# A two-layer decoder on one core: the last layer's first batch moved into the attention's pair loop, and two orders of the first layer changed

## The chip, the cores and the metric

One core of a Trainium2 chip runs the whole kernel in one launch. TensorE (PE) multiplies, VectorE (DVE), ScalarE (ACT) and GpSimd (POOL) work element by element, and SyncE (SP) starts the DMAs. Each engine takes its own instructions strictly in order, and they meet at semaphores. The metric is the time of one execution in device microseconds. Smaller is better.

## The reference, cut to what matters

The stream `x` is (2, 512, 128) in float32: two batches of 512 tokens, 1024 rows, kept as 8 tiles of 128 rows. Six sublayers follow one another, each with a residual sum and a layer norm:

```python
x = ln(x + gated_mix(x))                        # first layer, "a"
x = ln(x + cross_attention_and_ssm(x, ctx_768)) # "b": top 32 of 154 scores, FiLM, S4D by DFT, an FFN
x = ln(x + mha_and_moe(x))                      # "c": 8 experts, capacity 128
x = ln(x + attention(x))                        # last layer, "d": 16 heads of 64 in each batch, no mask
x = ln(x + latent_attention(ctx_768, x, mask))  # "e": 2 heads of 64, keys = 154 of the context + 512 of x
x = ln(x + top2_ffn(x))                         # "f": 4 live experts, hidden size 704

# d, in each batch:   z = softmax(q k^T / 8) v over 16 heads; y = x + concat(z) w_o
# e, in each batch:   ln_l = ln(x) * g + b; q, k, v = ln_l Wq^T, ln_l Wlkv^T;  the context gives 154 more k, v
#                     q, k: each head's row divided by its root mean square, times a gain
#                     softmax over 666 keys (masked ones of the context out), times v, times Wo^T, + bo
```

## The kernel before, in words

All data of a stage lies in SBUF at addresses planned by hand; `Space` hands out stretches and later stages reuse them. PSUM has 8 banks of 512 float32 columns, and `bank(i)` is bank i. The order on each engine is the order of the program text, and every hand-over is a named semaphore: `wait_ge(sem(name), n)` waits until it was raised n times. There is no planner.

**The first layer's b stage (L637 to L1060).** ScalarE writes angles in turns for the state-space kernel: 32 low lags and 16 high lags for each channel. VectorE rounds them (`b_dve_rounds`, L482 and L484), GpSimd subtracts (`b_pool_low_angles` in two halves, `b_pool_high_angles`), ScalarE takes the sine and cosine (`b_act_high_waves`, `b_act_low_waves`). Beside this, VectorE selects the 32 largest of 154 scores in 16 steps of two heads, and ScalarE feeds it with exponentials (`exponentials(j)`). GpSimd starts `b_pool_attention` with seven small operations on the FiLM row (`b_pool_film_rows`), then the marks, both low halves, the high angles, `u_n`, and then factors and modulated tiles in turn. `b_act_film_inputs` copies four products from PSUM between two exponentials. `taps_of_lags` on TensorE needs all factors, and everything of the state-space part follows it.

**The c stage (L1220 to L1525).** After the norm of the attention's output, the rows are transposed in two halves (`half_turn`), `logits` gives the gate, VectorE finds each row's expert, and `count_before` counts the rows ahead of it for the capacity. `expert(t)` multiplies tile t by all eight merged experts, in two halves of four experts each, `bias(t)` adds the biases, and `combine` on VectorE adds 128x128 blocks by their coefficients: 16 for two tiles. `rows_again(h)` turns the rows back, ScalarE copies them to `moe_sum`. GpSimd adds `n2_b` to the stream (`with_n2b`, L1432) right after the two reciprocal roots of the norm.

**The d stage (L1539 to L1817).** A pair is two heads of one batch; there are NP_ = 16, pairs 0 to 7 in batch 0. Step i of the loop holds the scores and exponentials of pair i, the rough maxima of pair i+1 (bf16 products whose row maximum becomes the shift of the exponent, written into a row of its own, `shift_in`), the projections of pair i+2, and the weighing and sums of pair i-1. Scores use banks 0 to 3, rough maxima 4 and 5, weighing 6, and projections and sums share bank 7. VectorE reduces four rough maxima, writes the shift row, takes the reciprocal of the sums (`unit`) and scales the weighed pair into `headed`. GpSimd adds the exponentials over keys (two half sums and a key sum for each pair). Step 16 only drains. Steps 14 and 15 also hold the turn and the product of the normed context. Behind the loop stand 64 products of the output projection, 8 pairs for each of 8 tiles (L1706).

**The e stage (L1821 to L2205).** Batch 0 first: residual sum and norm, a second norm, four transpositions, four latent projections of 384 columns, the norms of q and k rows (squares from ScalarE, `square_sums` and `scale` on VectorE, the power -1/2 on GpSimd, L1870), transpositions of q and k, casts to bf16, four rough maxima of 666 keys in four banks (1332 columns read), shift, then six chunks of scores and weighing. Batch 1's norm, projections, turns and maxima are put between batch 0's steps. The f stage's products start when the sums of batch 1 are on TensorE's queue (`hide`, L2243); their weights (4352 KB) come by a DMA that waits for the e stage's first stream norm, since they overwrite `value`.

## Time and profile before

| | |
|---|---|
| three runs | 701.97, 703.33, 707.58 us; median 703.33 |
| the profiled execution | 701.16 us, its span 699.4 us |
| TensorE, matmul | 614.9 us busy, 88% of the span |
| TensorE, weight load | 310.2 us, 44%, beside the matmuls |
| VectorE | 442.6 us, 63% |
| ScalarE | 288.4 us, 41% |
| GpSimd | 251.8 us, 36% |
| mean granted clock of TensorE | 0.943 of full speed |

A float32 product of a 128x512 tile is two matmul records. The granted clock is 1.00 or 0.50, which are 2.4 and 1.2 GHz. The chain that ended last is TensorE for 60% of the span, VectorE for 20%, GpSimd for 11%. The b stage runs to about 160 us, the c stage to 235, the d stage's loop starts at 249.6, the output projection at 470.6, and the f stage's first product at 555.9.

### The profile page before, as it was taken

What the parts mean: (1) busy time and instruction counts of PE and PEld (TensorE: products, weight loads), DVE (VectorE), ACT (ScalarE), POOL (GpSimd) and SP (SyncE); (2) the same over time, 40 slices, a digit from 0 to 9 for tenths busy, and PEclk for the clock granted to TensorE, in tenths of its full rate; (3) what the DMA queues carried; (4) which work ended last, traced back from release to release, by engine and by line L of the source; (5) the groups of instructions that cost most, each with busy time, mean ns of one, the idle gap of its engine ahead of it and who ended that gap; (6) DMA issues with size and microseconds to landing.
All of it is one profiled execution on the core that took longest, in us unless ns stands there. A gap on an engine that the chain in (4) does not pass through costs nothing.

```text
span 699.4 us, 8759 instructions
## 1 busy us (share of the span) xinstructions
PE 614.9 (88%) x3153; PEld 310.2 (44%) x3153; DVE 442.6 (63%) x1170; ACT 288.4 (41%) x548; POOL 251.8 (36%) x180
## 2 busy tenths in 40 slices
PE   7764869999797989999999999988568999999996
PEld 4322557876563322222222222328222346665655
DVE  6997997457739746676677667646743773333234
ACT  7969967032320564444444444420423342212120
POOL 2794652332601526446544554642435100000001
PEclk9956979999988999999999999999969999999998
DMA  8200014030000000000000000000600000000001
GB/s 319 88 0 0 2 66 178 1 121 1 1 0 1 0 0 1 1 0 1 1 1 1 0 1 0 1 1 0 256 0 1 0 1 1 0 1 0 1 0 31
DMA packets 3681, 18.92 MB, mean 27 GB/s; under 512 B 917, under 2 KB 2198, under 8 KB 3126
## 3 DMA queue, kind: packets, MB, share of 16 engines
q1 hardware_dynamic: 3638, 18.36, 6.9%
q8 instruction: 25, 0.41, 0.2%
q14 instruction: 18, 0.15, 0.1%
HBM read 17.84 MB, written 0.52 MB: 26 GB/s over the span
## 4 chain that ended last, share of the span: by engine, by line
PE 60%; DVE 20%; POOL 11%; issue 5%; ACT 4%; POOLq 0%; DVEq 0%; ACTq 0%
PE PS L2243 10%; PE PS L1607 8%; PE PS L2257 6%; DVE SB L1781 6%; PE PS L1591 5%; PE PS L1552 4%; PE PS L1575 3%; POOL SB L238 2%; PE PS L1623 2%; DVE SB L212 2%; DVE SB L199 2%; PE PS L1965 2%; DVE SB L1503 1%; PE PS L1976 1%; POOL SB L516 1%
## 5 line engine op out<-in xcount | busy, mean ns | idle before, releaser
L1767 POOL TENSOR_TENSOR SB<-SB 128x1024 f32<-128x1024 f32 x32 | 75.2, 2350 | 108.1 <-ACT SB L1730 108.0
L1781 DVE TENSOR_REDUCE SB<-PS 128x2 f32<-128x1024 f32 x64 | 78.5, 1226 | 55.0 <-PE PS L1575 54.9
L1730 ACT ACTIVATE SB<-PS 128x1024 f32<-128x1024 f32 x64 | 65.5, 1023 | 101.8 <-PE PS L1594 101.7
L2243 PE MATMUL PS<-SB 128*128 128x512 f32 x176 | 83.1, 609 | 0.2 <-DVE SB L2320 0.2
L1591 PE MATMUL PS<-SB 64*128 64x512 f32 x256 | 68.9, 616 | 1.1 <-ACT SB L1734 1.1
L1607 PE MATMUL PS<-SB 128*64 128x512 f32 x256 | 67.8, 610 | 1.2 <-DVE SB L1815 1.2
L2295 ACT ACTIVATE SB<-PS 128x512 f32<-128x512 f32 (+1 forms) x48 | 28.5, 595 | 92.0 <-PE PS L2243 89.0
L1811 DVE RECIPROCAL SB<-PS 128x512 f32<-128x512 f32 x16 | 53.7, 3358 | 17.6 <-PE PS L1623 17.6
L238 POOL TENSOR_TENSOR SB<-SB 128x4 f32<-128x4 f32 x18 | 19.6, 1092 | 120.9 <-DVE SB L204 120.9
L2320 DVE TENSOR_TENSOR SB<-SB,PS 128x512 f32<-128x512 f32 (+1 forms) x48 | 32.7, 687 | 48.1 <-PE PS L2243 43.7
L2257 PEld LDWEIGHTS PS<-SB 128*128 128x128 f32 (+1 forms) x384 | 49.4, 190 | 18.5 <-issue 10.0
L2257 PE MATMUL PS<-SB 128*128 128x128 f32 (+1 forms) x384 | 54.5, 285 | 1.4 <-DVE SB L2320 1.4
L244 POOL TENSOR_TENSOR SB<-SB 128x4 f32<-128x4 f32 (+1 forms) x6 | 5.5, 920 | 132.4 <-DVE SB L182 132.2
L2243 PEld LDWEIGHTS PS<-SB 128*128 128x128 f32 x176 | 31.1, 190 | 33.0 <-issue 27.7
L1552 PE MATMUL PS<-SB 128*128 128x512 f32 x64 | 37.5, 673 | 1.2 <-ACT SB L1713 0.7
L1771 POOL TENSOR_TENSOR SB<-SB 128x1024 f32<-128x1024 f32 x16 | 37.6, 2348 | 1.3
L1591 PEld LDWEIGHTS PS<-SB 64*128 64x128 f32 x256 | 22.0, 188 | 28.3 <-issue 23.5
L1607 PEld LDWEIGHTS PS<-SB 128*64 128x64 f32 x256 | 14.3, 135 | 42.8 <-issue 33.0
L2351 DVE SCALAR_TENSOR_TENSOR SB<-PS,SB 128x128 f32<-128x128 f32 x32 | 11.2, 351 | 30.3 <-PE PS L2257 30.3
L1575 PE MATMUL PS<-SB 64*128 64x512 bf16 x128 | 24.8, 384 | 4.6 <-DVE SB L1781 4.6
L1575 PEld LDWEIGHTS PS<-SB 64*128 64x128 bf16 x128 | 6.2, 93 | 47.0 <-DVE SB L1781 40.4
L1722 ACT ACTIVATE SB<-PS 128x512 bf16<-128x512 f32 x32 | 19.1, 597 | 17.5 <-PE PS L1552 17.5
(392 smaller groups left out, 1131.6 us busy)
## 6 DMA issues: line engine op xcount, KB each, us to landing
SB<-exp SPq DMA_DIRECT2D x1, 4352.0 KB, 13.8
SB<-moe SPq DMA_DIRECT2D x1, 4096.0 KB, 12.2
SB<-dft SPq DMA_DIRECT2D x1, 2304.0 KB, 11.7
SB<-att SPq DMA_DIRECT2D x1, 2048.0 KB, 7.9
SB<-mix SPq DMA_DIRECT2D x1, 768.5 KB, 4.4
SB<-mix SPq DMA_DIRECT2D x1, 640.0 KB, 5.5
SB<-ssm SPq DMA_DIRECT2D x1, 602.0 KB, 6.6
SB<-lat SPq DMA_DIRECT2D x1, 585.0 KB
```

Source lines behind the costliest of these rows:

```text
L238: pool.tensor_tensor(rstd[:, a:z], variance[:, a:z], minus_half[:, a:z], ALU.pow).then_inc(sem("norm_rstd"), 1)
L1552: pe.matmul(bank(b), w[:, 128 * pair:128 * pair + 128], xsT[:, 512 * batch:512 * batch + 512], start=True, stop=True)\
L1575: ins = pe.matmul(bank(4 + h), qb_ring[i % 3][head(h), 128 * qt:128 * qt + 128], kb_ring[i % 3][head(h), :], start=True, stop=True)
L1591: pe.matmul(bank(2 * (n % 2) + h), k_ring[i % 3][head(h), 128 * u:128 * u + 128], q_ring[i % 3][head(h), :], start=True, stop=False)
L1607: ins = pe.matmul(bank(6)[head(h), :], v, expd[i % 2][:, 1024 * kt + 512 * h:1024 * kt + 512 * h + 512], start=(kt == 0), stop=(kt == 3))
L1730: act.activation(expd[i % 2][:, 1024 * u:1024 * u + 1024], bank(2 * (u % 2), 2), ACT.Exp).then_inc(sem("d_exp"), 1)
L1767: pool.tensor_tensor(half_sums[half], e[:, 0:1024], e[:, 1024:], ALU.add).then_inc(sem("d_half_sum"), 1)
L1771: pool.tensor_tensor(key_sum, half_sums[0], half_sums[1], ALU.add).then_inc(sem("d_key_sum"), 1)
L1781: dve.tensor_reduce(shift[i % 2][:, qt:qt + DK + 1:DK], two_heads(bank(4, 2)), AX_X, ALU.max, negate=True)\
L1811: dve.reciprocal(unit, bank(7)).then_inc(sem("d_unit"), 1)
L2243: pe.matmul(bank(2 * (i % 3) + side), exp_w["e_w13"][:, c:c + 128], xsT[:, 512 * n:512 * n + 512], start=True, stop=True).then_inc(sem(("t ...
L2257: ins = pe.matmul(bank(6 + j % 2)[:, 0:128], hidden[e % 2][0:m, T * k + 128 * t:T * k + 128 * t + 128], w2, start=(k == 0), stop=(k == FCH ...
```

## The change

Three parts. In the last layer, batch 0's output projection goes into steps 10 and 11 of the pair loop (BESIDE = PAIRS + 2 = 10), two tiles in each, and the context's turn, the latents' turn, the context product and batch 0's latent projections go into steps 12 to 15; the norms and row norms that belong to them go into VectorE's and GpSimd's queues there. The drain step is written out and batch 1's output projection is mixed with batch 0's rough maxima. These take three banks in place of four: 512 keys of x in a bank of its own for each head, and the 154 context keys of both heads in the bank between. Batch 1's projections and maxima stand inside and behind batch 0's scores. The sums of batch 0 have three parts: GpSimd adds chunks 0 to 2, VectorE chunks 3 and 4. The weight DMA waits for the last weighing of the d stage. In the b stage the FiLM rows on GpSimd and two of four copies on ScalarE go behind the angles and waves. In the c stage the experts are ordered by halves around the count, and `with_n2b` waits for the norm.

The b stage, ScalarE and GpSimd (`b_act_rest_inputs` is the last four lines of `b_act_film_inputs`):

```diff
+    def b_act_rest_inputs(act):
...
         b_act_high_waves(act)
         b_act_low_waves(act)
+        b_act_rest_inputs(act)
         attn_in(act, 0)
...
         pool.wait_ge(sem("norm_rstd"), 2)
+        b_pool_marks(pool, follow)
+        b_pool_low_angles(pool, 0)
+        b_pool_high_angles(pool)
+        b_pool_low_angles(pool, 1)
+        pool.wait_ge(sem("s_low_products"), 3)
         b_pool_film_rows(pool, follow)
-        b_pool_marks(pool, follow)
-        for h in range(2):
-            b_pool_low_angles(pool, h)
-        b_pool_high_angles(pool)
...
         b_pool_high_factor(pool, follow, 0)
-        modulate(0)
         b_pool_high_factor(pool, follow, 1)
         b_pool_high_factor(pool, follow, 2)
+        modulate(0)
```

The c stage, TensorE and GpSimd:

```diff
         logits(0)
+        pe.wait_ge(sem("c_merged_in"), 5)
+        expert(0, (0,))
+        logits(1)
+        expert(0, (1,))
         rows_again(0)
-        logits(1)
-        pe.wait_ge(sem("c_merged_in"), 5)
-        expert(0)
-        rows_again(1)
+        expert(1, (0,))
         count_before()
-        expert(1)
+        expert(1, (1,))
         pe.wait_ge(sem("c_bias_row"), 1)
         bias(0)
         bias(1)
+        rows_again(1)
+        pe.wait_ge(sem("g_coef"), 1)
+        expert(3)
+        bias(3)
         pe.wait_ge(sem("c_y1_in"), 2)
         expert(2)
         bias(2)
-        pe.wait_ge(sem("g_coef"), 1)
-        expert(3)
-        bias(3)
...
         project(0, 0, 4)
+        pe.wait_ge(sem("c_added"), 5 * E0)
+        expert(7, (1,))
+        bias(7, (1,))
         pe.wait_ge(sem("c_added"), 6 * E0)
         project(0, 1, 3)
-        expert(7, (1,))
-        bias(7, (1,))
...
+        pool.wait_ge(sem("c_normed"), 1)
         for k in range(2):
             half = slice(4 * k, 4 * k + 4)
             pool.tensor_tensor(tiled(with_n2b)[:, half], tiled(xs)[:, half], four("n2_b"), ALU.add).then_inc(sem("c_kept"), 1)
```

The d stage, TensorE. In step 12 `beside` turns the context and in 13 the latents, both into bank 7; `beside_read` waits until bank 7 was read. The last pair's four products of the output projection close the block:

```diff
+        def beside(i):
+            pe.wait_ge(sem("d_unit"), i - 1)
+            if i < BESIDE + 2:
+                pe.wait_ge(sem("d_headed"), PAIRS)
+                for t in (2 * (i - BESIDE), 2 * (i - BESIDE) + 1):
+                    for pair in range(PAIRS):
+                        ins = pe.matmul(bank(7)[:, 128 * t:128 * t + 128], headed[:, 512 * pair + 128 * t:512 * pair + 128 * t + 128],
+                                        att["w_o"][:, 128 * pair:128 * pair + 128], start=(pair == 0), stop=(pair == PAIRS - 1))
+                ins.then_inc(sem("d_out"), 1)
...
+        def beside_read(i):
...
             for u in range(4):
...
                 if ahead and u < 2:
                     maxima(i + 1, 2 * u)
+                if slot and u == 0:
+                    beside(i)
+                elif i + 2 < NP_ and u < 2:
                     project(i + 2, u)
+                if i == NP_ - 2 and u < 2:
+                    context(u)
                 if i == NP_ - 1 and u < 2:
-                    context(u)
+                    e_project(pe, 2 * u)
+                    e_project(pe, 2 * u + 1)
+                if i == NP_ - 1 and u == 3:
+                    e_turn_tiles(pe, 0)
+                    e_turn_tiles(pe, 1)
                 if before:
                     weigh(i - 1, u)
+                if slot and u == 0:
+                    beside_read(i)
+                    project(i + 2, 0)
...
+        last = NP_ - 1
+        e_turn_ctx(pe)
+        weigh(last, 0)
+        weigh(last, 1)
+        e_maxima(pe, 0, 0)
+        weigh(last, 2)
+        weigh(last, 3)
+        e_maxima(pe, 0, 1)
+        sums(last)
+        pe.matmul(bank(0), zeros_low, mask_16[0:1, 0:512], start=True, stop=False)
+        attended_part((0, 1))
+        e_maxima(pe, 0, 2)
+        attended_part((2, 3))
+        e_maxima(pe, 0, 3)
+        pe.wait_ge(sem("d_headed"), NP_)
```

The d stage, GpSimd and VectorE (ScalarE copies the turns, the context product and the projections at the same steps, each ahead of `rows_in` or behind `exp`):

```diff
+            if i == NP_ - 1:
+                for k in range(3):
+                    e_pool_row_norms(pool, k)
             for half in range(2):
+                if half and BESIDE < i <= BESIDE + 2:
+                    pool_rstd_half(pool, 0)
...
                 maximum(i + 1, 0)
+                if BESIDE <= i < BESIDE + 2:
+                    c = slice(256 * (i - BESIDE), 256 * (i - BESIDE) + 256)
+                    dve.wait_ge(sem("d_out"), i - BESIDE + 1)
+                    dve.scalar_tensor_tensor(xsum[:, c], xs[:, c], 2.0, bank(7)[:, c], ALU.mult, ALU.add)\
+                       .then_inc(sem("e_attended"), 1)
                 maximum(i + 1, 1)
+                if i == BESIDE + 1:
+                    dve.wait_ge(sem("e_attended"), 2)
+                    norm_stats(dve, follow, tiled(xsum), 0)
                 maximum(i + 1, 2)
                 maximum(i + 1, 3)
                 shift_in(i + 1)
+            if i == BESIDE + 1:
+                norm_apply(dve, tiled(xsum), tiled(xs), 0).then_inc(sem("stage_half"), 1)
+            if i == BESIDE + 2:
+                norm_apply(dve, tiled(xs), tiled(xn), 0).then_inc(sem("e_half"), 1)
+            if i == NP_ - 1:
+                e_dve_rows(dve, follow)
+            if i >= 1:
+                unit_of(i - 1)
+            if i == BESIDE + 1:
+                dve.wait_ge(sem("stage_half"), 4)
+                norm_stats(dve, follow, tiled(xs), 0)
```

The e stage. `e_maxima` makes two products of 512 columns and four of 154. Batch 1's six chunks follow `shifts(1)` in the same way, with `out(0)` at u = 1. VectorE's queue behind the loop is: casts, maxima 0 and 1 of batch 0, `headed_of(15)`, maxima 2 and 3, and then the last lines here:

```diff
-        sp.wait_ge(sem("stage_done"), 4)
+        sp.wait_ge(sem("d_weighed"), NP_)
...
+    def rough_at(b, qt):
+        return 512 * (1 if b == 0 else 0 if qt % 2 else 5)
+    def e_maxima(pe, b, qt):
...
+        if b == 0 and qt or b == 1 and qt >= 2:
+            pe.wait_ge(sem("d_max"), 4 * NP_ + n - b)
...
         shifts(0)
+        score(0, 0)
         for u in range(KT):
+            if u + 1 < KT:
+                score(0, u + 1)
+            if u == 2:
+                turn_half(pe, tiled(xn), "e_normed", 1, 1, 5)
+            weigh(0, u)
+            if u == 3:
+                e_project(pe, 4)
+                e_project(pe, 5)
+            if u == 4:
+                e_project(pe, 6)
+                e_project(pe, 7)
+        e_turn_tiles(pe, 2)
+        e_turn_tiles(pe, 3)
+        for qt in range(4):
+            e_maxima(pe, 1, qt)
+        sums(0)
         shifts(1)
...
+    def e_dve_rows(dve, follow):
+        follow(dve.tensor_scalar(q_gain, lat["qn_g"], DK ** -0.5, None, ALU.mult))
+        follow(dve.tensor_tensor(e_own, ident[:, 0:4], ident[:, DK:DK + 4], ALU.add))
         dve.wait_ge(sem("e_ctx_kv_in"), 2)
+        follow(dve.tensor_tensor(ctx_squares.rearrange("p (i w) -> p i w", i=4), e_ck, e_ck, ALU.mult))
+        e_square_sums(dve, follow, ctx_squares, 32, 8)
+        e_row_norms(dve, follow, 0)
         dve.wait_ge(sem("e_rnorm"), 1)
+        e_scale(dve, e_ck, 4, 2, 32)
+        e_row_norms(dve, follow, 1)
+        e_rows_scaled(dve, 0)
+        e_rows_scaled(dve, 1)
...
+        dve.scalar_tensor_tensor(xsum[:, c], xs[:, c], 2.0, bank(0), ALU.mult, ALU.add).then_inc(sem("e_attended"), 1)
+        norm_stats(dve, follow, tiled(xsum), 1)
         shift_in(0)
+        norm_apply(dve, tiled(xsum), tiled(xs), 1).then_inc(sem("stage_done"), 1)
```

## Rows read from the trace of the kernel before

**Rows 1.** Busy time by stretch, TensorE: stretch, length, busy (records), granted clock, DMA, GB/s.
```profile
249.50:387.00 137.50, 131.85 (x568) 1.00 0.00 1
455.20:556.00 100.80, 79.44 (x431) 0.92 0.11 45
497.30:500.30 3.00, 2.97 (x8) 0.50 0.89 383
507.30:521.00 13.70, 8.96 (x38) 0.50 0.00 1
```
**Rows 2.** Timeline, TensorE, loop steps 13 to 15: start, length, engine, line, operation, count.
```profile
424.37 1.13 PE L1591 MATMUL PS<-SB 64*128 64x512 f32 x4
...
438.16 1.13 PE L1591 MATMUL PS<-SB 64*128 64x512 f32 x4
...
450.79 1.13 PE L1591 MATMUL PS<-SB 64*128 64x512 f32 x4
```
**Rows 3.** Timeline, TensorE: the output projection, and the f stage's first product.
```profile
470.64 14.56 PE L1706 MATMUL PS<-SB 128*128 128x128 f32 x128
...
555.87 3.68 PE L2243 MATMUL PS<-SB 128*128 128x512 f32 x8
```
**Rows 4.** Timeline, VectorE and GpSimd, 447 to 503 us; in brackets the idle time before.
```profile
447.76 3.36 DVE L1811 RECIPROCAL SB<-PS 128x512 f32<-128x512 f32 x1 [0.33 <-PE PS L1623]
...
453.42 2.35 POOL L1771 TENSOR_TENSOR SB<-SB 128x1024 f32<-128x1024 f32 x1
...
478.09 0.69 DVE L2083 SCALAR_TENSOR_TENSOR SB<-SB,PS 128x512 f32<-128x512 f32 x1 [4.89 <-PE PS L1706]
...
480.45 1.41 POOL L238 TENSOR_TENSOR SB<-SB 128x4 f32<-128x4 f32 x1 [12.59 <-DVE SB L204]
...
492.22 1.64 POOL L1870 TENSOR_TENSOR SB<-SB 128x8 f32<-128x8 f32 x1 [2.16 <-DVE SB L2096]
...
494.23 0.75 DVE L2090 TENSOR_TENSOR SB<-SB 128x256 f32<-128x256 f32 x2
...
501.48 1.55 DVE L2141 TENSOR_REDUCE SB<-PS 128x2 f32<-128x1332 f32 x1 [1.27 <-PE PS L1949]
```
**Rows 5.** Timeline, ScalarE and GpSimd in the b stage.
```profile
34.55 1.08 ACT L643 ACTIVATE SB<-PS 124x512 f32<-124x512 f32 x2
...
48.74 1.91 ACT L547 ACTIVATE SB<-SB 128x2048 f32<-128x2048 f32 x1 [3.37 <-POOL SB L489]
...
82.09 4.59 POOL L516 TENSOR_TENSOR SB<-SB 128x2048 f32<-128x2048 f32 x1 [5.21 <-ACT SB L534]
```
**Rows 6.** Timeline, GpSimd and VectorE around VectorE's two roundings.
```profile
26.19 3.03 POOL L650 TENSOR_SCALAR SB<-SB 32x256 f32<-32x256 f32 x1
26.68 2.28 DVE L482 TENSOR_SCALAR SB<-SB 128x4096 f32<-128x4096 f32 x1
...
29.42 1.38 DVE L484 TENSOR_SCALAR SB<-SB 128x2048 f32<-128x2048 f32 x1 [0.45 <-ACT SB L475]
```
**Rows 7.** Timeline, GpSimd's two sums and VectorE's norm beside them in the c stage.
```profile
189.28 2.50 POOL L1432 TENSOR_TENSOR SB<-SB 128x512 f32<-128x512 f32 x2
...
189.35 1.29 DVE L212 TENSOR_SCALAR SB<-SB 128x128 f32<-128x128 f32 x1
...
190.56 1.73 DVE L212 TENSOR_SCALAR SB<-SB 128x128 f32<-128x128 f32 x1
```
**Rows 8.** Busy time by stretch, TensorE, in the c stage; columns as in rows 1.
```profile
189.90:192.60 2.70, 0.02 (x1) 1.00 0.00 0
193.40:200.10 6.70, 6.70 (x23) 0.50 0.00 0
```
**Rows 9.** Timeline, VectorE's combination and TensorE's expert products.
```profile
205.47 8.49 DVE L1503 SCALAR_TENSOR_TENSOR SB<-PS,SB 128x128 f32<-128x128 f32 x32 [2.22 <-PE PS L1322]
...
207.32 1.88 PE L1314 MATMUL PS<-SB 128*128 128x512 f32 x4
...
228.54 2.16 DVE L1503 SCALAR_TENSOR_TENSOR SB<-PS,SB 128x128 f32<-128x128 f32 x8 [1.73 <-PE PS L1322]
```

More of the change, by code:

```diff
@@ L1672, in d_pe @@
         pe.wait_ge(sem("d_v_in"), NT)
-        for i in range(NP_ + 1):
-            now, ahead, before = i < NP_, i + 1 < NP_, i >= 1
+        for i in range(NP_):
+            ahead, before, slot = i + 1 < NP_, i >= 1, BESIDE <= i < BESIDE + 4
             for u in range(4):
-                if now:
-                    score(i, u)
+                score(i, u)
                 if ahead and u == 2:
@@ new lines, in d_pe @@
+        e_turn_ctx(pe)
[12 more added lines that the diff above has]
+        pe.wait_ge(sem("d_headed"), NP_)
+        for t in range(4):
+            ins = pe.matmul(bank(0)[:, 128 * t:128 * t + 128], headed[:, 512 * last + 128 * t:512 * last + 128 * t + 128],
+                            att["w_o"][:, 128 * (PAIRS - 1):128 * PAIRS], start=False, stop=(t == 3))
@@ L1850, in e_pool_masks @@
         follow(pool.memset(mask_16, 0.0))
+        follow(pool.memset(ctx_16, 0.0))
         by_chunk = lambda a: a.rearrange("p (b c) -> p b c", b=B)
@@ L1882, in e_pool @@
             .then_inc(sem("e_kept"), 1)
[L1884 to L1889 removed]
+        for k in (3, 4):
+            e_pool_row_norms(pool, k)
         for k in range(2):
```

451 lines of the change are left out of this document (214 added, 237 removed).

## The prediction

> **What bounds the kernel now.** I read the busy time by stretch first [rows 1]: in the pair loop TensorE is busy 131.85 of 137.50 us, so whatever is put into that loop costs its full length. From 455.2 to 556 us, the end of the attention and the whole latent attention, it is busy 79.44 of 100.80: 21.4 us idle. Two pieces of that stretch ran at half clock, 2.97 and 8.96 us of work; half of them, 6.0 us, is lost too. So 27.4 us could be had there. Then the timelines: the scores of successive steps of the loop start 13.79 us apart with both projections, 12.63 us in step i = 14, which has none but the context's turn [rows 2]. The output projection is 14.56 us without a gap, all 8 tiles behind the last pair; the last stage's first product starts at 555.87 [rows 3]. In the first layer three places matter. ScalarE waits 3.37 us for angles from GpSimd, and GpSimd later 5.21 us for ScalarE's rates [rows 5]. The second half of a norm is held up, and TensorE's clock falls behind it [rows 7, 8]. VectorE waits 1.73 us for the last expert product [rows 9]. The sum is made against the profiled execution, 701.16 us (span 699.4); the median of the three runs is 703.33, 2.2 us higher.
>
> **First layer, angles** (`b_pool_attention`, `b_act_attention`). GpSimd's film rows, about 7.6 us of small operations ahead of the angle subtractions, go behind them, so the one that the waves wait for ends near 40 instead of 48.7. ScalarE has its last exponential behind it at 48.74 - 3.37 = 45.37, so the waves start there: 3.37 us gained. The rest inputs, 1.08 us [rows 5], now stand between the waves and the next exponentials, for which VectorE waits: 2.3 us net. The rates, and GpSimd's product at 82.09 that waited 5.21 us for them, come as much earlier, and so do the taps and all that follows. `modulate(0)` goes behind two factors; its reader starts at 80 and GpSimd is done by 70, so that wait costs nothing as long as those 10 us last. The moved row chain ends near 52 and the film product wants it at 57: covered by 5 us.
> Who holds the ports matters here. While VectorE ran its 2.28 us rounding, a 32x256 operation of GpSimd lasted 3.03 us and ended 0.26 behind it; VectorE's second rounding then came out at 1.38 us [rows 6]. In the new order GpSimd's first subtraction, a 4.5 us operation, may start as soon as the first rounding ends at 28.96, 0.46 before the second is ready. I take it that the marks' memset, which falls at 26.6, pushes the first rounding back by up to 0.9 us, so that the second follows directly and wins; GpSimd then waits and has the time. The other outcome is rival 1.
>
> **First layer, experts** (`c_pe`, `c_pool`). GpSimd's `with_n2b` sums (2.50 us) lie on top of the second half of a norm: VectorE's tensor_scalars last 1.29 and 1.73 us there [rows 7], the four 3.3 us instead of about 1.1. The new wait for `c_normed` moves the sums behind: 2.1 us. Behind that gap of 2.7 us TensorE ran 6.7 us at half clock [rows 8]; the gap shrinks to 0.6 us, so I take full clock: 3.4 us more. `rows_again(1)`, 0.45 at full clock, leaves the way to the combination. Its start [rows 9]: 205.47 - 2.1 - 3.4 - 0.45 = 199.5, 6.0 us earlier. Behind it `rows_again(1)` and two experts, 1.88 us and a bias of 0.4 each, need 5.0 us where VectorE is back after 16 x 0.27 = 4.3: 0.6 lost. In the tail expert 7's second half moves ahead of a projection and VectorE's wait of 1.73 falls by 1.0; what is late next is that projection and the values behind it, which had 0.6 us to spare and follow at full clock: I take 0.9. Sum 6.3; if the clock falls all the same, 2.9.
>
> **Last layer.** TensorE's work stays, but its place changes. Into steps 10 and 11 go two tiles each of batch 0's output projection, 14.56/4 = 3.64 us; into 12 the context's turn, into 13 the latents' turn, into 14 the context product (about 1.1 us each half, where 12.63 had room for none), into 15 four latent projections and eight transposes. Step 15 starts 11 us later, paid in full, and what stood behind the loop is as much shorter. New are a third part of `sums(0)` and a zero product: 1.1 us. So the gain is the 27.4 us less the waits of the new order, which I followed through the queues:
> - Steps 11 and 12: the norm's statistics (478.09 to 480.45 less 0.69 for the residual sum [rows 4]: 1.7) delay the third maximum by 0.5; the apply (1.1) puts off the reciprocal and, with the second statistics, the next first maximum by 0.8. 1.3 us.
> - Step 15: VectorE's row chain queues behind GpSimd's half sum and key sum (2.35 us each, to 5.0 us into the step), since its small two-operand products contend with them. Then squares, three powers of 1.64 and scales of 0.75 for two tiles [rows 4]: `e_scaled` reaches 3 at 12.9, and TensorE is there at 11.5. 1.4 us. On GpSimd's queue the powers stand ahead of pair 15's own sums, which end at 19.3 when `sums(15)` wants them at 23: covered by 4 us.
> - The reciprocal of pair 14 (3.36 us [rows 4]) now queues behind that chain and `weigh(15, 0)` waits for it: 1.8 us.
> - VectorE's casts to bf16 fall on GpSimd's key sum of pair 15 and wait for its end: 1.7 us; without contention nothing.
> - Three banks allow one set of maxima; the last ends at 33.6 us, behind a reciprocal. Then residual sum 0.69, statistics 1.7 and the shift row 0.7 stand before the first score: 3.4 us idle in all. On VectorE both norm steps are ahead of the shift row, and TensorE has nothing else queued.
> - Batch 1's rows: behind the last projection come two copies, a reduce, a power of 1.64, two scales of 0.75, transposes, two copies and a cast, with one transposition beside them: 5.0 us.
> - Batch 1's maxima (1.55 us each [rows 4]) in two sets: 3.1 us. Its shift row: 0.8.
> Together 18.5 us. The clock falls once more behind the last two; with 5 us of work at half speed, 2.5. Gain 27.4 - 18.5 - 2.5 - 1.1 = 5.3 us. Bounds: without contention and without the fall 5.3 + 3.5 + 2.5 = 11; with falls as long as before and a third as long again 5.3 - 9 = -4. I take the inner value, since gaps and work like those of [rows 1] recur. The weight stream (4352 KB) now starts behind pair 15's weighing, some 60 us ahead of its reader; it cost nothing visible before.
>
> **Sum.** 2.3 + 6.3 + 5.3 = 13.9: 687.3 in the profiled frame, 689.4 in that of the median. I say 688.
>
> **A rule that speaks against it.** In the rows either engine waits until the other's operation has ended [rows 6, 7]. The Trainium skill, page SBUF — State Buffer, section SBUF: two separate sides, makes it a rule: one pair of ports is locked for a whole instruction, by a GpSimd operation or by a VectorE operation in a two-port mode or with two SBUF operands. The trace agrees in both groups. By that rule the casts and products of step 15 block fully, as in the sum above; without it the sum would be 3.5 us lower, 684.
>
> **Rivals.**
> 1. GpSimd's first subtraction wins at 28.96. The second rounding waits until 33.5 and all selection starts 3.8 us late; the exponential ahead of the waves ends at 49.2 instead of 45.4, and 2.3 gained turn into 1.4 lost: 691. For it speaks the order of the queues, against it the memset. It is the page's lock applied to one operation. Chance 0.13.
> 2. The clock falls in the c stage anyway: 691. Against it, only the 2.7 us gap of [rows 8] preceded a fall here. Chance 0.12.
> 3. The last layer gains nothing or loses a few us: step 15 becomes a VectorE chain and each block goes the wrong way. 692 to 697. That the moved work fills no idle time, so that the change doesn't do what it says, is this case too. Chance 0.18.
> 4. The other side: TensorE stays at half clock from the gap before batch 1's maxima to the last stage, as it did from 507.3 to 521 [rows 1]. 27 us of work stand there; the gain of 13.9 is used up once 28 us run at half speed, and one fall more in the first batch gives that: 704 to 712. Against it, steady work ended the fall in [rows 8] after 6.7 us. Chance 0.05.
> 5. More than forecast, no contention and no fall: 679 to 683. Chance 0.09.
> The forecast keeps 0.43, with a range of its own of 684 to 692.
>
> **Numbers.** Range 681 to 697: the forecast, cases 1 and 2, most of 3, half of 5. Within 1% of 703.3 (about what a measurement can't tell from no change) is 696.3 to 710.4. Faster 0.83; same 0.12, from the end of 3 and part of 4; slower 0.05.
>
> **What would show it.** ScalarE's first wave near 45.4; the combination starting near 197 (199.5 less 2.3) with full clock before it; steps 10 and 11 at 17.4 us and a little more; TensorE waiting for `e_scaled` and for the reciprocal in step 15; about 52 us from the latent attention's first score to the last stage's first product, with one stretch of half clock. I am wrong if VectorE's second rounding ends behind 31.5, if a step from 10 to 14 takes over 18.5 us, or if TensorE idles more than 20 us from step 15's start to the last stage.

## The result, and the profile after

The changed kernel takes 697.45 us, median of 9 runs (694.02 to 699.16), the kernel before 703.49 in the 9 runs beside them: ratio 0.9903, 95% interval 0.9875 to 0.9931 (the quotient of the two medians is 0.9914). It is faster by 1%, where I had forecast 688 and a range of 681 to 697. The profiled execution is 697.45 us with a span of 695.7, against 701.16 and 699.4. One execution of e3 (913.19 us) and one of e17 (1494.49 us, its profiled one, so that no trace of e17 is read) were disturbed and are left out of the figures below.

I read the after trace at four marks: the first score of the pair loop, the first scores of steps 10 and 15, the first score of the latent attention, and the last stage's first product. The table gives the distances (the last mark is here the 128x4 routing product, 0.92 us ahead of the 128x512 one of [rows 3]).

| | first score of the loop | step 10 to step 15 | step 15 to latent score | latent score to last stage |
|---|---|---|---|---|
| before | 249.60 | 67.77 | 65.16 | 39.00 |
| after | 241.30 | 81.93 | 41.02 | 53.63 |

From the first score of the loop to step 10 it is 133.4 us in both. So the first layer brought 8.3 us, where the forecast had 8.6, and the last layer lost 4.65 where it had a gain of 5.3. All but 0.3 us of the error is in the last layer.

The first layer, after: timeline of VectorE, GpSimd and ScalarE; start, length, engine, line, operation. The rows answer to [rows 5] and [rows 6].

```profile
26.97 2.99 POOL L688 MEMSET SB<- 32x1024 f32 x1
29.48 1.57 DVE L484 TENSOR_SCALAR SB<-SB 128x2048 f32<-128x2048 f32 x1 [0.41 <-ACT SB L475]
30.05 5.38 POOL L494 TENSOR_TENSOR SB<-SB 128x2048 f32<-128x2048 f32 x1
...
45.30 1.89 ACT L547 ACTIVATE SB<-SB 128x2048 f32<-128x2048 f32 x1
```

The first wave comes at 45.30 without a wait (forecast 45.4), GpSimd's product of [rows 5] at 79.63, 2.46 us earlier (forecast 2.3). VectorE's second rounding won the ports, with 1.57 us, but not in the way that I had forecast. The first rounding was not pushed back; it lasted from 26.79 to 29.07, and the memset, which began 0.18 us behind it, took 2.99 us instead of the 0.95 of the kernel before. That kept GpSimd until 29.96, half a microsecond behind the start of the second rounding. In the experts' stage the norm's eight tensor_scalars are short again, GpSimd's sums wait for them (they start at 188.01), and the combination begins at 197.09, where the forecast had 197.2; these rows answer to [rows 7] and [rows 9]:

```profile
185.57 2.36 DVE L212 TENSOR_SCALAR SB<-SB 128x128 f32<-128x128 f32 x8
...
187.98 0.66 PE L1240 MATMUL PS<-SB 128*128 128x128 f32 x4 [0.60 <-DVE SB L212]
...
197.09 4.23 DVE L1512 SCALAR_TENSOR_TENSOR SB<-PS,SB 128x128 f32<-128x128 f32 x16 [1.36 <-PE PS L1327]
```

TensorE from step 10 to the last stage, before and then after: stretch, length, busy (records), granted clock, DMA, GB/s. The three rows at 0.50 are the stretches at half clock, to be read against [rows 1]; the last is the experts' stage, which answers to [rows 8].

```profile
383.02:555.87 172.85, 148.66 (x734) 0.95 0.07 26
```
```profile
374.69:552.20 177.51, 156.41 (x743) 0.94 0.06 26
...
473.90:480.65 6.75, 5.37 (x16) 0.50 0.00 1
497.90:501.10 3.20, 3.20 (x10) 0.50 0.00 0
521.83:531.95 10.12, 8.64 (x34) 0.50 0.01 2
189.00:200.00 11.00, 10.95 (x55) 1.00 0.00 0
```

Idle time fell from 24.2 to 21.1 us: 3.1 gained, where the forecast had 2.9 (21.4 less 18.5). But half of the work at half clock is now 17.21/2 = 8.6 us, before it was 6.0, and the work itself, counted at full clock, grew from 142.7 to 147.8. So 3.1 - 2.6 - 5.1 = -4.6.

The new waits, after: timeline of steps 11 and 12 on GpSimd, VectorE and TensorE, then step 15.

```profile
402.24 2.35 POOL L1832 TENSOR_TENSOR SB<-SB 128x1024 f32<-128x1024 f32 x1 [5.02 <-ACT SB L1785]
402.45 2.17 DVE L204 TENSOR_SCALAR SB<-SB 128x4 f32<-128x4 f32 x1
...
405.80 0.39 PE L1585 MATMUL PS<-SB 64*128 64x512 bf16 x2 [2.06 <-DVE SB L1846]
...
414.56 2.34 POOL L1836 TENSOR_TENSOR SB<-SB 128x1024 f32<-128x1024 f32 x1
414.87 2.06 DVE L204 TENSOR_SCALAR SB<-SB 128x4 f32<-128x4 f32 x1
...
418.11 0.39 PE L1585 MATMUL PS<-SB 64*128 64x512 bf16 x2 [1.86 <-DVE SB L1846]
...
467.48 4.82 POOL L1832 TENSOR_TENSOR SB<-SB 128x1024 f32<-128x1024 f32 x2
467.55 5.04 DVE L2178 TENSOR_TENSOR SB<-SB 128x256 f32<-128x256 f32 x2 [1.19 <-POOL SB L1957]
...
472.73 0.63 PE L2007 MATMUL PS<-SB 128*128 128x128 f32 x4 [3.50 <-DVE SB L2178]
```

A 128x4 operation that takes 0.17 us elsewhere takes 2.17 and 2.06 when it begins 0.2 or 0.3 us behind one of GpSimd's sums, and TensorE waits 2.06 and 1.86 for the maximum behind it. In step 15 the last two scales, 0.75 us in [rows 4], take 5.04, because both half sums of pair 15 started 0.07 us before them; TensorE waits 3.50, its clock falls behind that, and it waits 1.38 more for the reciprocal that comes behind the scales.

The second batch's rows and maxima on TensorE, after:

```profile
497.64 2.00 PE L2063 MATMUL PS<-SB 64*128 64x512 f32 x4 [2.37 <-DVE SB L2230]
...
518.01 0.63 PE L2007 MATMUL PS<-SB 128*128 128x128 f32 x4 [1.54 <-DVE SB L2178]
...
522.40 0.61 PE L2040 MATMUL PS<-SB 64*128 64x512 bf16 x2 [1.82 <-DVE SB L2218]
...
528.18 4.62 PE L2092 MATMUL PS<-SB 128*64 128x512 f32 x12 [0.21 <-DVE SB L2225]
...
533.84 1.13 PE L2063 MATMUL PS<-SB 64*128 64x512 f32 x4 [0.79 <-DVE SB L2230]
```

A third wait of 1.32 us stands between the first two. Of the sums at 528.18, the first 3.8 of 4.62 us run at half clock.

### The profile page after: what moved, and what is told of

Read it like the earlier page. It is cut to its first block, busy times and chain, and to the rows that moved or that the text cites. A ratio compares the mean times of both kernels' runs of the same rounds, so it can differ in the third digit from the quotient of the medians.

```text
span 695.7 us, 8771 instructions
## 1 busy us (share of the span) xinstructions
PE 617.9 (89%) x3161; PEld 307.6 (44%) x3162; DVE 451.1 (65%) x1172; ACT 287.3 (41%) x548; POOL 246.7 (35%) x178
## 4 chain that ended last, share of the span: by engine, by line
PE 62%; DVE 20%; ACT 9%; issue 5%; POOL 4%; POOLq 0%; DVEq 0%; ACTq 0%
PE PS L2339 10%; PE PS L1617 8%; PE PS L2353 6%; DVE SB L1846 6%; PE PS L1562 4%; PE PS L1601 4%; PE PS L1585 3%; PE PS L1687 2%; PE PS L1631 2%; PE PS L2063 2%; DVE SB L199 2%; PE PS L2074 1%; DVE SB L1868 1%; ACT SB L468 1%; POOL SB L238 1%
## 5 line engine op out<-in xcount | busy, mean ns | idle before, releaser
L1617 PE MATMUL PS<-SB 128*64 128x512 f32 x256 | 69.9, 628 | 1.4 <-DVE SB L1871 1.4
L2353 PEld LDWEIGHTS PS<-SB 128*128 128x128 f32 (+1 forms) x384 | 49.4, 190 | 18.5 <-issue 10.0
## 6 DMA issues: line engine op xcount, KB each, us to landing
SB<-moe SPq DMA_DIRECT2D x1, 4096.0 KB, 12.3
```

Source lines behind the costliest of these rows:

```text
L1617: ins = pe.matmul(bank(6)[head(h), :], v, expd[i % 2][:, 1024 * kt + 512 * h:1024 * kt + 512 * h + 512], start=(kt == 0), stop=(kt == 3))
L2353: ins = pe.matmul(bank(6 + j % 2)[:, 0:128], hidden[e % 2][0:m, T * k + 128 * t:T * k + 128 * t + 128], w2, start=(k == 0), stop=(k == FCH ...
```

## The experiments

**The two layers apart.** e1 is the kernel before with the first layer's edits alone, e2 with the last layer's alone (the diff shown ahead, cut between `c_pool` and `d_projection`).

e1. 

> The kernel before with only the first layer's two orders changed (angles and experts); the last layer is the old one. Theory A, from the trace after (the first score of the last layer's loop starts 8.3 us earlier, the whole span is only 3.7 us shorter): the first layer gives its 8.3 us undiminished, about 693 us in the profiled frame, ratio near 0.988. Rival B: the first layer's gain is partly eaten further on whatever the last layer does (the loss is not the last layer's): as the changed kernel, about 697, ratio near 0.995.

e2. 

> The kernel before with only the last layer's part of the change. Theory A: the last layer loses 4.6 us by itself: about 705.8 in the profiled frame, ratio near 1.0065. Rival B: it loses only because of what the first layer does to it, so alone it changes nothing: 701. What I predicted of it was a gain of 5.3 (695.9).

Measured: e1 693.85, ratio 0.9856 (0.9788 to 0.9924); e2 707.94, ratio 1.0055 (1.0021 to 1.0089). The product, 0.9910, is the changed kernel's 0.9903. In e1's trace the loop's first score stands at 241.18, so the first layer's gain is there without the last layer's edits. Step 10 to the last stage takes 67.76 + 66.40 + 39.29 = 173.45 us, 1.5 more than before with the same code, since the clock was down for 23.9 us of that way, before for 17.1. In e2's trace that way takes 177.2 us, 5.2 more than before. Theory A holds in both: the last layer's part makes the kernel slower by itself.

**VectorE's small operation beside GpSimd's sum.** e3 moves GpSimd's two powers:

```diff
-                if half and BESIDE < i <= BESIDE + 2:
-                    pool_rstd_half(pool, 0)
+            if i == BESIDE + 1: pool_rstd_half(pool, 0)    # ahead of both half sums
...
+            if i == BESIDE + 1: pool_rstd_half(pool, 0)    # ahead of the key sum
```

> The changed kernel with GpSimd's two powers of steps 11 and 12 moved: each stands ahead of the 128x1024 sum that ran beside VectorE's small variance operation (the first ahead of step 11's half sums, the second ahead of its key sum). Theory A: VectorE's 128x4 tensor_scalar took 2.17 and 2.06 us because GpSimd's sum was running; with no sum beside it it takes about 0.17, TensorE's waits of 2.06 and 1.86 fall to 0.25 each, and the kernel is 3.4 us faster than the changed one (694.0). Rival B: the operation is slow of itself in that place (follows an aggregate, other cause), or the delayed sums come late for the products that need them: no change, 697.5.

Measured 693.97, ratio 0.9847 (0.9784 to 0.9909). The trace of e3, VectorE and TensorE:

```profile
415.80 0.17 DVE L204 TENSOR_SCALAR SB<-SB 128x4 f32<-128x4 f32 x1
...
418.87 0.39 PE L1585 MATMUL PS<-SB 64*128 64x512 bf16 x2 [0.25 <-DVE SB L1848]
```

This one and the one at 405.36 take 0.17 us, and step 10 to step 15 takes 78.07 instead of 81.93: 3.86 less. Theory A holds. What is left over before, 78.07 - 67.77 = 10.3 us, is the products put in (7.54 of the output projection, 0.6 and 2.1 of turn and context): these steps have no other cost once VectorE isn't held.

**The scales of step 15.** e4 has one line more, ahead of pair 15's half sums:

```diff
                 for k in range(3):
                     e_pool_row_norms(pool, k)
+                pool.wait_ge(sem("e_scaled"), 3)
```

> The changed kernel with one wait more: GpSimd begins pair 15's half sums only when VectorE has scaled the rows of tiles 2 and 3. Theory A: those two 128x256 products took 5.04 us because GpSimd's two half sums held the ports; now 0.76, TensorE's wait of 3.50 us in step 15 all but goes, and with it the fall of the clock at 473.9 (6.7 us at half clock, 2.7 us lost): 697.5 - 3.5 - 2.7 = 691.3. Rival B: the block only moves: the two casts and the narrow copies now fall on GpSimd's sums and take 2 to 5 us, so that the first maxima are late by as much: 695 to 697.5. Rival C: the clock falls all the same: 694.

Measured 695.03, ratio 0.9859 (0.9807 to 0.9911). Step 15 to the latent score: 36.82 instead of 41.02, 4.2 less; 0.6 of it goes again up to the last stage (54.22 instead of 53.63), where the clock is down for 13.65 us instead of 10.24. The trace of e4:

```profile
467.43 0.76 DVE L2179 TENSOR_TENSOR SB<-SB 128x256 f32<-128x256 f32 x2 [1.19 <-POOL SB L1958]
468.10 3.35 DVE L1869 RECIPROCAL SB<-PS 128x512 f32<-128x512 f32 x1
...
468.26 4.67 POOL L1833 TENSOR_TENSOR SB<-SB 128x1024 f32<-128x1024 f32 x2 [0.87 <-DVE SB L2179]
...
473.01 2.42 POOL L1837 TENSOR_TENSOR SB<-SB 128x1024 f32<-128x1024 f32 x1
...
473.14 2.58 DVE L2219 CAST SB<-SB 128x512 bf16<-128x512 f32 x1
...
476.44 0.39 PE L2041 MATMUL PS<-SB 64*128 64x512 bf16 x2 [1.75 <-DVE SB L2246]
```

A and B both hold in part. The scales take 0.76 us and the first fall of the clock is gone; the second cast now lies behind the key sum and takes 2.58 us instead of 0.42. Note the reciprocal: it reads PSUM, and beside two half sums it takes its 3.35 us.

**The second batch's sums.** e5 moves the first batch's 12 sum products ahead of batch 1's maxima, into bank 3; e11 leaves two of their three parts out of the computation.

```diff
+        sums(0)                           # e5, writes bank 3; batch 1's second score goes to banks 6 and 7
         e_turn_tiles(pe, 2)
...
-        sums(0)
```
```diff
-                parts = [weight_sum[0], late_sum]
+                parts = []                # e11
```

e5. 

> The changed kernel with the first batch's sums of weights (12 products, 4.62 us at half clock behind the second batch's maxima) moved into the idle time ahead of those maxima, into a bank that is free there; the second score of batch 1 goes to two other banks. Theory A: they fill idle time (1.54 + 1.32 + 1.82 us of waits there) and leave the way of the shift row: 3 us faster (694.5). If the fall of the clock behind those waits comes from the idleness, it is also shorter (10.1 us of stretch before), up to 4.3 us more: 690 to 692. Rival B: the row chain of VectorE, GpSimd and ScalarE sets the pace and the reciprocal of these sums is late for the first output: 697.

e11. 

> The changed kernel with one part of three in the first batch's sums (4 products of 128x512 instead of 12; two parts of the sum are left out of the computation). Theory A: the change has made this sum 8 products longer (it was 4 before), and I had counted 4 of them; they stand on TensorE's way at half clock: 4.62 us become 1.54, 3.1 us faster: 694.4. Rival B: the clock comes back later by as much, since there is less work ahead of the shift row: 1 to 2 us, 696.

Measured: e5 697.27, ratio 0.9914 (0.9887 to 0.9940); e11 696.47, ratio 0.9896 (0.9853 to 0.9939). Neither can be told from the changed kernel by its median. In the traces the way from the latent score to the last stage is 52.47 in e5 and 52.86 in e11, against 53.63. In e5 batch 1's first score comes 32.8 us behind batch 0's instead of 36.2, and 2.2 of these 3.4 us go again: the clock now falls behind the maxima and is still down during the scores. In e11 the same happens (B): its first score of batch 1, which lasts 1.13 us at full clock, takes

```profile
532.46 2.08 PE L2063 MATMUL PS<-SB 64*128 64x512 f32 x4 [0.78 <-DVE SB L2230]
```

**The repaired kernel.** e6 joins e3, e4 and e5 with a wait of GpSimd's key sum for VectorE's casts, and one of its first angle subtraction for the second rounding. e18 is the same kernel again; e10 is e6 without e5's move.

```diff
+            if i == NP_ - 1: pool.wait_ge(sem("e_qk_16"), 4)
             pool.tensor_tensor(key_sum, half_sums[0], half_sums[1], ALU.add)
...
         b_pool_marks(pool, follow)
+        pool.wait_ge(sem("s_rounds"), 2)
         b_pool_low_angles(pool, 0)
```

e6. 

> The changed kernel with five edits: the two powers moved off VectorE's variance operations; pair 15's half sums behind the scales of the rows; pair 15's key sum behind VectorE's casts and narrow copies (in the run with the held half sums one cast took 2.58 us beside them); the early sums of batch 0; and GpSimd's first subtraction of the angles behind the second rounding. Theory A, the effects add: 3.4 + 4.2 + 1.7 + 3 = 12.3 us under the changed kernel, 685; TensorE's waits in steps 11 and 12 are 0.25 us, in step 15 at most 1.6. Rival B: the held key sum makes the sums of pair 15 late, and its reciprocal the third maxima: 688 to 690.

e10. 

> The kernel with all five edits less one: the sums of batch 0 stand behind the second batch's maxima again. Theory A: the early sums were worth 1.2 us (in the traces of the two kernels that differ in them alone, the way from the first score to the last stage is 52.5 against 53.6 us; 3.4 us gained at the shift row, 2 given back by half clock behind it): 688.1. Rival B: nothing: 686.9.

e18. 

> The kernel with all five edits once more, without fillings, on the chip of the other two: 686.9 as before; step 10 to step 15 78.07 us, step 15 to the first score 35.00, from there to the last stage 52.1. If those three stand, they don't depend on the run, and the spread between runs comes from the first layer.

Measured: e6 686.92, ratio 0.9772 (0.9750 to 0.9794); e10 688.14, ratio 0.9781 (0.9739 to 0.9823); e18 687.65, ratio 0.9792 (0.9774 to 0.9810). The marks of e6: 78.07, 35.00, 52.09; of e18: 78.07, 34.99, 52.94; of e10: 78.08, 35.01, 53.32. The last layer of e6 takes 165.16 us (the sum of the three), 11.4 less than in the changed kernel. Of these, 3.9 (e3), 4.2 (e4, up to the latent score) and 1.2 (e5) were measured apart; the other 2.1 are a difference, put down to the held key sum, which no run has alone. The whole kernel gains 9.2 us by the ratios and 10.5 by the medians, where I had forecast 12.3. The sums of pair 15 do not come late. Against the kernel before the last layer is 6.8 us shorter: the forecast's 5.3 was there to be had, with four edits more. The early sums are worth 0.4 to 1.2 us. I was wrong that the last stretch doesn't depend on the run: it did by 0.85.

**The experts' wait.** e7 is the changed kernel without `pool.wait_ge(sem("c_normed"), 1)`.

> The changed kernel without the new wait that holds GpSimd's sums (with_n2b) back until the norm's second half is applied. Theory A, my step for the experts: the four tensor_scalars take 3.3 us again instead of 1.1, TensorE idles longer for the turn, and its clock falls behind it as it did before: 2.1 + 3.4 = 5.5 us slower, 703. Rival B: only the contention comes back, 2.1: 699.5. Rival C: the other moves of that stage alone keep TensorE fed, no change: 697.5.

Measured 705.35, ratio 1.0025 (0.9997 to 1.0054), 7.9 us behind the changed kernel. Timeline of e7, then two stretches of its TensorE as above:

```profile
185.64 4.51 DVE L212 TENSOR_SCALAR SB<-SB 128x128 f32<-128x128 f32 x8
...
190.20 0.96 PE L1240 MATMUL PS<-SB 128*128 128x128 f32 x4 [2.74 <-DVE SB L212]
```
```profile
187.46:190.20 2.74, 0.00 (x0) 1.00 0.00 0
190.60:200.60 10.00, 10.00 (x31) 0.50 0.00 0
```

Theory A, and more than it: GpSimd's sums start at 186.82, on top of the norm; an idle 2.74 us instead of 0.60, then 10 us at half clock, where the kernel before had 6.7 [rows 8]. The loop's first score comes at 248.43 instead of 241.30. One wait of GpSimd's is worth 7.1 us here, nearly all that the first layer gained.

**The race for the ports at 29 us.** e12 starts GpSimd's subtraction as early as it can (marks behind it), e8 holds it back until the second rounding is done.

e8. 

> The changed kernel with one wait more: GpSimd's first subtraction of the angles starts only when VectorE's second rounding is done. In the profiled run of the changed kernel VectorE won anyway (its rounding 1.57 us); in one later run of a sister kernel GpSimd won and the rounding took 5.47 us, the waves came at 48.81 instead of 45.30 us, and the first scores 3 us later. Theory A: the race goes now this way, now that, and the wait takes the bad outcome away: waves at 45.3 in the profile, median 697 or up to 1 us less, the spread narrower than 694.0 to 699.2. Rival B: the bad outcome is rare or belongs to that kernel: 697.5, spread as before.

e12. 

> The changed kernel with GpSimd's first subtraction of the angles ahead of the marks (and their memset), so that it starts the moment the first rounding is done. Theory A, my rival 1 made certain: VectorE's second rounding waits for it (5.4 us instead of 1.5), the selection is 3.8 us late, the waves start near 49 instead of 45.3: 3.0 to 3.7 us slower than the changed kernel, 700.5 to 701.2. Theory B: the second rounding is early enough all the same, or the marks behind save as much: 697.5.

Measured: e12 699.31, ratio 0.9942 (0.9921 to 0.9962); e8 697.78, ratio 0.9914 (0.9885 to 0.9943). First the trace of e12, then that of e3, whose first layer is the changed kernel's:

```profile
28.71 4.52 POOL L494 TENSOR_TENSOR SB<-SB 128x2048 f32<-128x2048 f32 x1 [3.50 <-DVE SB L482]
...
29.42 4.90 DVE L484 TENSOR_SCALAR SB<-SB 128x2048 f32<-128x2048 f32 x1 [0.84 <-ACT SB L475]
```
```profile
29.27 4.51 POOL L494 TENSOR_TENSOR SB<-SB 128x2048 f32<-128x2048 f32 x1
...
29.39 5.47 DVE L484 TENSOR_SCALAR SB<-SB 128x2048 f32<-128x2048 f32 x1 [1.09 <-ACT SB L475]
...
48.81 1.90 ACT L547 ACTIVATE SB<-SB 128x2048 f32<-128x2048 f32 x1
```

My rival 1 is real. In e3 it happened by itself, decided by 0.12 us, and in e15, below, once more, by 0.07 us. Eight traces have the changed kernel's code in that place; GpSimd won in these two, VectorE in the other six, once by only 0.10 us (e5). So which engine wins changes from run to run, and it was in part luck that the profiled run of the changed kernel had the forecast's side. The loop's first score comes at 243.9 to 244.4 us where GpSimd won (e12, e3, e15) and at 241.2 to 242.4 where VectorE did (the changed kernel, e1, e4, e5, e11): a cost of 1.5 to 3.2 us.

Holding GpSimd back brings no gain that can be seen. In e8 the first wave comes at 46.59 and the first score at 242.31, but not because the angles came late: GpSimd's high angles were ready at 40.43, and ScalarE came to the wave without a pause behind its exponentials, as it did in e5 at 46.77 without the new wait. The first layer has other spread of this size: in e14, which has the wait, the first score came at 244.25. Whether the wait narrows the spread, four runs (694.41 to 698.47) can't tell.

**Half clock.** What does it cost end to end? In e15 the changed kernel gets products that nobody reads in TensorE's waits; e9, e13, e14, e16 and e17 are e6 with such fillings. The numbers are products of 128x512 (fp32) ahead of the first latent score, ahead of batch 1's maxima, and behind them: e9 4, 3, 3; e13 4, 3, 1; e14 4, 3, 0; e16 2, 2, 1; e17 2, 2, 0.

```diff
         shifts(0)
+        stay_warm(pe, 2, 5, q_T[0])                      # e16
         score(0, 0)
...
         e_turn_tiles(pe, 3)
+        stay_warm(pe, 2, 1, weights[0][:, 0:512])
         for qt in range(4):
             e_maxima(pe, 1, qt)
+        pe.wait_ge(sem("d_max"), 4 * NP_ + 7)
+        stay_warm(pe, 1, 5, weights[0][:, 0:512])
```

e15. 

> The changed kernel with unread products in TensorE's waits alone: 4 of 128x512 (fp32) ahead of the first score of batch 0, and 3, 2 and 3 around the two turns of batch 1's rows. Nothing else is changed. Theory A: the idleness makes the falls at 497.9 (1.6 us lost) and 521.8 (4.3 us lost); filled, both vanish and the way from the first score to the last stage is 4 to 6 us shorter: 692 to 693.5. Rival B: the clock falls in that stretch for another reason (the thin work of the maxima): 696 to 697.5. Rival C: the filling itself is late by as much as it saves: 697.5.

e9. 

> The kernel with all five edits (686.9) and products whose results nobody reads, put into TensorE's three waits of the latent attention: 4 of 128x512 (fp32) ahead of the first score of batch 0, 3 ahead of batch 1's maxima, 3 behind them. Theory A: the clock falls behind these waits because TensorE idles in them (2.38 us before the first fall at 488, 1.82, 0.95 and 1.67 us around the second at 515.5 to 525); filled, the falls vanish and 5.2 us lost to half clock come back: 682 to 683. Rival B: the fall has another cause, or only moves to a later place: 686 to 687. Rival C: the extra products end behind the data that the next products wait for and cost their own time: 688 to 690.

e13. 

> The kernel with all five edits and the unread products, but 1 instead of 3 behind batch 1's maxima. Theory A: these three took 4.23 us, partly at half clock, and held the shift row and the next score back by about 2.5 us; with one the clock stays up and the score comes 2.5 us sooner: 684.0 to 684.5. Rival B: the clock falls there and takes it back: 686.

e14. 

> The same with none behind the maxima. Theory A: the waits of 0.7, 1.7 and 0.8 us behind batch 1's maxima bring one fall of the clock, 2 us of work lost: 685.5. Rival B: no fall, since the products ahead of the maxima have filled the longest wait: 683.5 to 684.

e16. 

> The kernel with all five edits and unread products that fit the waits: 2 of 128x512 (fp32) ahead of the first score (1.8 us in a wait of 2.38), 2 ahead of batch 1's maxima (1.83 us in one of 1.82), 1 behind them. Theory A: clock kept costs nothing now and gives back what the overrun took: the first score comes 35.0 us behind step 15's start (36.0 with four products) and the last stage 51.4 or less behind it: 1.3 to 2 us faster than without the fillings, 685. Rival B: the part of the clock that matters is small, since VectorE's reductions set the pace there: within 0.5 us.

e17. 

> The same with none behind the maxima. Theory A: one fall of the clock behind the maxima, as in e14 (E0 to the last stage 52.04 there, less 0.8 for the overrun): 0.5 to 1 us faster than without fillings, 686. Rival B: within 0.5 us.

Measured: e15 697.02, ratio 0.9909 (0.9879 to 0.9938); e9 686.77, ratio 0.9767 (0.9717 to 0.9817); e13 686.56, ratio 0.9750 (0.9719 to 0.9782); e14 688.03, ratio 0.9771 (0.9741 to 0.9801); e16 685.26, ratio 0.9755 (0.9735 to 0.9774); e17 686.93, ratio 0.9783 (0.9761 to 0.9805). Theory A missed by 2 to 5 us in e15, e9, e13 and e14, and held in e16 and e17. Beside e18 on the same chip e16 is 2.4 us faster and e17 0.7. The stretch from the latent score to the last stage, TensorE, first of the changed kernel, then of e15, of e6 and of e16 (up to the 128x512 product):

```profile
497.64:552.20 54.56, 47.95 (x206) 0.87 0.00 1
```
```profile
502.04:555.62 53.58, 50.58 (x223) 0.97 0.00 1
```
```profile
488.70:541.70 53.00, 47.12 (x205) 0.87 0.00 1
```
```profile
488.56:540.14 51.58, 47.81 (x211) 0.93 0.00 1
```

The waits do make the falls: filled, the clock's mean rises from 0.87 to 0.97, and one fall of 3.4 us is left. But of the 5.9 us of half clock there (half of 3.20 + 8.64) e15 took 4.4 away, and that was worth 1.0 us up to the last stage. The filling ahead of the latent score cost as much, since it overran its wait (the transposition of the shift to the score is 3.69 us, in the changed kernel 2.70). The trace shows why the gain is so small. VectorE's four reductions of the maxima take 5.90 us in both kernels, and the sums behind them start 30.5 us after the latent score in both; slow products lay beside the reductions. All that is gained is in the sums, 4.62 us in the changed kernel and here in e15:

```profile
532.56 3.67 PE L2092 MATMUL PS<-SB 128*64 128x512 f32 x12 [0.21 <-DVE SB L2229]
```

The median of e15 is the changed kernel's within 0.5 us; its profiled run, 700.93, had lost the race at 29 us and one stretch of clock in the pair loop (421.73 to 425.14). Overruns cost the same elsewhere: in e9, e13 and e14 step 15 to the latent score is 36.0 instead of 35.0. The trace of e16 shows fillings that fit:

```profile
486.01 1.88 PE L264 MATMUL PS<-SB 128*128 128x512 f32 x4
...
488.56 1.13 PE L2070 MATMUL PS<-SB 64*128 64x512 f32 x4 [0.67 <-DVE SB L2240]
...
509.85 1.88 PE L264 MATMUL PS<-SB 128*128 128x512 f32 x4
...
517.14 2.07 PE L264 MATMUL PS<-SB 128*128 128x512 f32 x2 [0.69 <-DVE SB L2235]
```

The latent score now runs at full clock, and the kernel has the lowest median, with a ratio level with e13's: 0.9755 against 0.9903, some 10 us below the changed kernel. Its last layer is 8.2 us shorter than before (164.65 against 172.85), 2.3 shorter than in e18 and 1.4 shorter than in e6. Fillings that fit gave back over half of the half clock that they took away: 2.3 us for 4.0 against e18, 1.4 for 2.4 against e6. One fall is left, behind the maxima.

## Why the prediction was wrong

**The first layer was right by its steps, but for one.** Waves, GpSimd's product and combination came within 0.3 us of their forecast times; no clock fell ahead of the combination. The step that was wrong is the memset: it did not push the first rounding back, the rounding held it, and with six of eight traces on the forecast's side the right time was partly luck. In the experts' tail VectorE's wait of 1.73 became 0.48. e7 shows that the two effects which I priced at 2.1 and 3.4 us are one chain and are worth 7.1, and e12, e3 and e15 price rival 1 at 1.5 to 3.2 instead of 3.7.

**The failed step: what VectorE's small operations cost beside GpSimd's sums.** The last layer's idle time was right in sum, not in parts. Forecast 18.5 us of waits. Measured on TensorE: steps 11 and 12 3.9 (forecast 1.3), the scales 3.5 (1.4), the reciprocal 1.4 (1.8), the casts 0 (1.7), ahead of the first score 3.1 (3.4), batch 1's rows 4.7 (5.0), maxima and shift row 1.7 (3.9): 18.3. That the sums agree is chance: 4.7 us too little in the first two places stand against 4.9 too much in the others. I had let GpSimd's sums block VectorE's products and casts of step 15, but not the 128x4 operation in the norm's statistics in steps 11 and 12, for which I counted only its 0.17 us of length. And in step 15 I set the row chain behind GpSimd's sums of pair 14 and looked at pair 15's only from GpSimd's side ("covered by 4 us"); the power that frees VectorE's scales frees these sums too, and GpSimd was ahead by 0.07 us. e3 and e4 show both: 3.9 and 4.2 us. The text had named it as a sign of being wrong that "a step from 10 to 14 takes over 18.5 us": step 11 took 19.68.

**The work was mis-sized.** I added 1.1 us for "a third part of `sums(0)` and a zero product". It is 5.1. The sum had one part before and has three now, so two were added (1.9 us). A set of maxima took 0.43 us from product to product (521.11 to 521.54 in the trace before), with two heads side by side in each pair of 64-row products; the four 128x154 products of the new layout use all rows and come one by one: 0.69 us (480.77 to 481.46), 2.1 us over eight sets. The projection cut into pieces costs 0.7 more, the zero product 0.3.

```profile
521.11 0.31 PE L1945 MATMUL PS<-SB 64*128 64x333 bf16 x2
521.25 0.45 PE L1949 MATMUL PS<-SB 64*128 64x333 bf16 x4
521.54 1.02 PE L1965 MATMUL PS<-SB 64*128 64x512 f32 x4
```
```profile
480.77 0.39 PE L2040 MATMUL PS<-SB 64*128 64x512 bf16 x2
481.09 0.24 PE L2044 MATMUL PS<-SB 128*128 128x154 bf16 x1
...
481.46 1.94 PE L1617 MATMUL PS<-SB 128*64 128x512 f32 x8
```

**Half clock was forecast at 2.5 us and measured at 8.6.** I put one fall behind the last two waits; there were three, one of them behind the scales. So the sum is 27.4 + 2.8 idle in the steady loop before, 21.1 idle after, 8.6 and 5.1: 30.2 - 21.1 - 8.6 - 5.1 = -4.6.

**The sum was an identity, not a chain.** Idle, slow and busy time of one engine do add up, but removing one term does not give its size back: e15 took 4.4 us of half clock away for 1.0, e11 8 products for 0.8. What could be had was at the blocked VectorE operations (3.9 + 4.2, and 1.8 for the cast that is blocked once the scales are freed), which the idle term held without naming them. Read as an identity, the miss of 9.9 us is 4.0 of work and 6.1 of half clock, with the idle time 0.2 better. Read by the experiments, removing the two blocks gives 8.1 in e3 and e4; the forecast had itself allowed 1.3 and 1.4 as waits there, so they explain 5.4 beyond it. The two readings overlap, since part of the half clock lies behind the scales' wait; how they divide is argued, not shown. Rival 3 had this outcome ("step 15 becomes a VectorE chain"), 692 to 697, at 0.18; the time lies 0.45 us above the range. In the profiled frame its upper end, 697, leaves room for a loss of 4.4 us behind the first layer's gain of 8.6; the last layer lost 4.65, and the first gained 0.3 less. My bounds for the last layer, 11 to -4, did not hold the -4.65 either.

**The rule of the ports.** The Trainium skill, page SBUF — State Buffer, section SBUF: two separate sides, has the lock for a whole instruction. The traces agree: 128x4 in 2.17 us, two scales in 5.04, a cast in 2.58, GpSimd's own subtraction in 5.38 beside VectorE's 1.57. I applied it to the operations that I had looked for and not to all. The start of a record does not say by itself who holds the ports: in [rows 6] GpSimd's 32x256 operation began 0.49 us before VectorE's rounding and was held all the same, 3.03 us; in the changed kernel, away from the rounding, it took 0.87.

## What to carry to other kernels

Where GpSimd runs long sums, list every VectorE operation with SBUF operands that falls on them, the tiny ones first, and order GpSimd behind them: a 0.17 us operation cost 2 us, twice, and one wait was worth 7.1 us. When the end of one operation frees both engines, 0.07 us can decide which is first, as in step 15, so write the order down. Don't price slow clock or extra products of an engine by their length where another engine sets the pace; ask what the next product waits for.

## What the runs showed of the hardware

- VectorE's operations that read PSUM were not held: the reciprocal took 3.35 us beside two half sums of GpSimd's in e4, and a maximum of e3 (407.14) 1.23 beside a sum that had started at 406.68.
- The port race at 29 us went to GpSimd in two of eight traces with the same code, by 0.12 and 0.07 us, and the loop's first score came 1.8 to 3.2 us later in them. With equal code in that place, step 15 to the latent score was 40.9 to 41.1 us in five traces, 40.2 in one and 39.3 in three, by how long the clock stayed down.
- 0.60 us of idle time left the clock up where 2.74 us brought 10 us at half clock; in the changed kernel 2.37 us brought 3.2 us.
